# Routing a mixture-of-experts stage by a token table made on the chip, with gathered rows, folded RMS weights and an early load of half of W2

## What is computed

```python
x = x + xattn(ctx, ctx, layernorm(x), mask, wq, bq, wk, bk, wv, bv, wo, bo)
# ffn on z = layernorm(x):
xn = z * rsqrt(mean(z*z) + 1e-6) * rms_w
scores = softmax(xn @ gate_w.T)                  # 8 experts
e, s = argmax(scores), max(scores)
y = silu(xn @ W1[e] + b1[e]) @ W2[e] + b2[e]     # 256 -> 1024 -> 256
x = x + y * s
```

## Time and profile before

| | us |
|---|---|
| median of 3 runs | 1009.69 |
| lowest and highest of them | 1008.04, 1959.81 |
| the profiled execution, its time | 1013.72 |
| the profiled execution, its span (first to last instruction) | 1012.0 |
| mean granted clock of TensorE | 0.957 |

### The profile page before, as it was taken

How to read it: one execution, slowest core, us unless ns; L and a number is a source line. 1 busy time by engine, 2 the same in 40 slices (tenths; PEclk the granted TensorE clock), 3 DMA queues, 4 the chain that set the end, 5 groups by cost and what they waited for, 6 DMA issues and landing times.

```text
span 1012.0 us, 31886 instructions
## 1 busy us (share of the span) xinstructions
PE 849.3 (84%) x9355; PEld 612.3 (61%) x9356; DVE 613.6 (61%) x1906; ACT 448.0 (44%) x1121; POOL 523.5 (52%) x766
## 2 busy tenths in 40 slices
PE   1789999999999999999999999930089999999995
PEld 0456666666666666666666666610077777778773
DVE  4467777777777777777777777441044444445442
ACT  0235555555555555555555555500033333334331
POOL 0355567567667667667667667436622222232221
PEclk9999999999999999999999999955589999999998
DMA  9746765775775775775775775345222122222210
GB/s 255 184 131 164 188 185 160 179 195 149 185 200 147 187 201 144 185 206 142 189 204 142 187 206 144 76 194 215 87 58 72 59 63 76 58 71 71 66 48 7
DMA packets 124528, 143.72 MB, mean 142 GB/s; under 512 B 13274, under 2 KB 116550, under 8 KB 123464
## 3 DMA queue, kind: packets, MB, share of 16 engines
q1 hardware_dynamic: 119048, 132.15, 48.6%
q0 software_dynamic: 4896, 11.05, 3.4%
q10 hardware_dynamic: 544, 0.00, 0.0%
HBM read 100.10 MB, written 44.89 MB: 143 GB/s over the span
## 4 chain that ended last, share of the span: by engine, by line
PE 32%; issue 18%; SPq 15%; DMA 13%; POOL 12%; DVE 6%; ACT 1%; POOLq 0%; DVEq 0%; ACTq 0%
PE ps L1163 13%; DMA arena_a<-in_x 12%; PE ps L1178 10%; SPq L404 4%; SPq L399 4%; POOL arena_a L550 3%; POOL arena_b L529 3%; POOL arena_b L530 3%; PE ps L980 2%; POOL arena_a L557 2%; POOL arena_b L509 1%; SPq L365 1%; PE ps L994 1%; DVE arena_b L1297 1%; SPq L444 1%
## 5 line engine op out<-in xcount | busy, mean ns | idle before, releaser
L1315 DVE CUSTOM_DVE_ANT_0 arena_a<-ps,arena_a 112x375 bf16<-112x375 f32 x256 | 140.5, 549 | 45.5 <-PE ps L916 38.3
L697 ACT ACTIVATE arena_a<-ps 119x448 f32<-119x448 f32 (+1 forms) x256 | 131.7, 540 | 71.9 <-PE ps L942 71.3
L1163 PE MATMUL ps<-arena_b,w_parts 128*128 128x128 f16 x1680 | 148.5, 227 | 5.3 <-issue 4.3
L938 PE MATMUL ps<-arena_a 128*128 128x448 bf16 x384 | 137.3, 357 | 8.0 <-DVE arena_a L1324 5.9
L1163 PEld LDWEIGHTS ps<-arena_b,w_parts 128*128 x1680 | 118.7, 98 | 37.2 <-issue 11.2
L1315 DVE CUSTOM_DVE_ANT_0 arena_b<-ps,arena_a 112x375 bf16<-112x375 f32 x256 | 139.8, 546 | 0.0
L942 PE MATMUL ps<-arena_a 128*128 128x224 f16 x768 | 136.8, 260 | 0.0
L831 ACT ACTIVATE arena_b<-ps,b_sb 128x128 f32<-128x128 f32 x280 | 79.4, 372 | 113.3 <-PE ps L1163 113.1
L655 POOL DMA_INDIRECT out<-arena_b x35 | 35.6, 1018 | 179.8 <-DVE arena_b L1479 131.2
L1497 DVE TENSOR_SCALAR arena_b<-arena_b 128x512 f16<-128x512 f32 x70 | 30.3, 433 | 129.2 <-ACT arena_b L831 91.4
L1178 PE MATMUL ps<-arena_a,arena_b 128*128 x840 | 97.5, 273 | 4.6 <-DVE arena_b L1500 3.8
(11 more groups left out here) (170 smaller groups left out, 1510.0 us busy)
## 6 DMA issues: line engine op xcount, KB each, us to landing
arena_a<-k_spill SPq DMA_DIRECT2D x128, 192.0 KB, 3.8
arena_b<-in_L_ffn_W SPq DMA_DIRECT2D x64, 256.0 KB, 4.3
arena_a<-q_spill SPq DMA_DIRECT2D x128, 112.0 KB, 4.4
k_spill<-arena_a SPq DMA_DIRECT2D x32, 384.0 KB, 4.7
arena_b<-in_ctx SPq DMA_DIRECT2D x32, 256.0 KB
w_spill<-arena_b SPq DMA_DIRECT2D x32, 256.0 KB, 4.5
arena_a<-w_spill SPq DMA_DIRECT2D x8, 1024.0 KB, 11.7
arena_a<-in_x SPq DMA_DIRECT2D x64, 112.0 KB, 4.6
```

What stands on the lines that cost most here:

```text
L697: nc.scalar.activation(probsT[u % PROB_BUFFERS][0:n], scoreT_bank[c][0:n, 0:QUAD * T], ACT.Exp, scale=1.0 / SCALE_SCORES).then_inc(probs_r ...
L938: pe.matmul(bank[:, 0:QUAD * T], mask_keys[:, quad, c, :], max_rows[par].rearrange("p h t -> p (h t)"), start=True, stop=False)
L1163: mm = pe.matmul(ps[:, 1 + 2 * parity + f // 4, (f % 4) * P:(f % 4 + 1) * P], w1_parts[:, w_part, bass.ds(e, 1), k, f * P:(f + 1) * P].rea ...
L1315: nc.vector.tensor_tensor_reduce(out=masked_scores[r % 2], in0=shared_bank[r][0:T, 0:S], in1=mask_bias, scale=-1.0, scalar=3.4e38, op0=ALU ...
```

## The change

- Attention no longer multiplies rows by the RMS weights. They are folded into W1's scale (`w1_scale`) and the gate weights at the start. `scale_routed` goes, and `routed_factor` has two operations in place of seven (a combined epsilon makes one rsqrt of two).
- Each batch's centred row and its x1 row lie side by side in `row_tile` and are spilled together (224 KB a batch) to `rows`, in step lag 3 after `centred_ready`, in place of x1 alone (112 KB) in lag 2.
- Nothing is sorted in memory: the zero fill, `xr_all`, the 32 scatters and SP's loads of sorted rows go. The slots are worked out by a new chain of 28 linked DVE operations; then 32 one-hot comparisons (one a batch) and 32 products on PE give, for each place of each tile, the token's number. The constants for it (36 POOL instructions) are made in step 32.
- In the FFN POOL's `gather` fetches the 2 KB rows (centred row and x1) straight into `xs`, the tile that PE transposes, by the token table; a second indirect DMA fetches the scores. The copy of two token columns stands ahead of them. SP loads only b2.
- Half of W2's split parts (experts 0 to 3, 4 MB) is loaded by SP after step 17, the rest behind attention as before. W2's place in memory is a new arena, so that its first half is free during attention.

The diff, cut to its core:

```diff
-def run_steps(eng, body):
+def run_steps(eng, body, midway=None):
...
-    with eng.Fori(0, (B - 2 - PEELED_FIRST) // UNROLL) as i:
+    first, steps = PEELED_FIRST, B - 2 - PEELED_FIRST
+    if midway is not None:
+        with eng.Fori(0, EARLY_STEPS // UNROLL) as i:
+            for k in range(UNROLL):
+                body(Step(first + k, i, True))
+        midway()
+        first, steps = first + EARLY_STEPS, steps - EARLY_STEPS
+    with eng.Fori(0, steps // UNROLL) as i:
...
-            sp.wait_ge(constants, N_CONST_POOL)
-            sp.dma_start(sorted_rows.rearrange("(n p) d -> p n d", p=P),
-                         zeros.unsqueeze(1).to_broadcast([P, FFN_TILES, ROW])).then_inc(zeroed, 16)
...
-                if st.exists(2):
-                    wait_apart(sp, x1_ready, st.batch(2) + 1, sp_passed)
-                    sp.dma_start(x1_rows[bass.ds(st.batch(2), 1)].rearrange("o t d -> t (o d)"),
-                                 x1[st.parity(2)]).then_inc(x1_spilled[st.parity(2)], 16)
-            run_steps(sp, step)
+                if st.exists(3):
+                    wait_apart(sp, centred_ready, st.batch(3) + 1, sp_passed)
+                    sp.dma_start(rows[:, bass.ds(st.batch(3), 1), :].rearrange("t o d -> t (o d)"),
+                                 row_tile[st.parity(3)]).then_inc(rows_spilled[st.parity(3)], 16)
+            def load_w2(first, chunks):
+                for part in range(2):
+                    for e in range(first, first + EARLY, 2):
+                        sp.dma_start(w2_parts[:, e:e + 2, part].rearrange("p e f d -> p e (f d)"),
+                                     w2_spill[:, part, e * chunks:(e + 2) * chunks].rearrange(
+                                         "p (e c) n -> p e (c n)", e=2)).then_inc(w2_loaded, 16)
+            def load_early_w2():
+                sp.wait_ge(w2_spilled, 16 * (PEELED_FIRST + EARLY_STEPS - 1))
+                load_w2(0, B // EXPERTS)
+            run_steps(sp, step, load_early_w2)
+            sp.wait_ge(score_ready, 1)
+            sp.dma_start(score_rows, top_score).then_inc(score_spilled, 16)
...
-            def scale_routed(st):
-                b = st.batch(3)
-                wait_count(pool, xrT_ready, b)
-                pool.wait_ge(centred_ready, b + 1)
-                pool.tensor_tensor(xr_now, centred, rmsw, ALU.mult).then_inc(xr_ready, 1)
-                pool.tensor_tensor(xr_all[:, bass.ds(b, 1), 0:D].rearrange("p o d -> p (o d)"),
-                                   centred, rmsw, ALU.mult).then_inc(xr_ready, 1)
...
-            for b in range(B):
-                pool.indirect_dma_start(out=sorted_rows, out_offset=bass.IndirectOffsetOnAxis(ap=slot_of[:, b:b + 1], axis=0),
-                                        in_=xr_all[:, b, :], in_offset=None).then_inc(scattered, 16)
...
-            def gather(t, buffer, first):
+            def gather(t, buffer, nth, first):
                 if not first:
+                    pool.wait_ge(out_stored[buffer], 16 * nth)
                     pool.wait_ge(out_ready, t + 1 - FFN_UNROLL)
-                wait_apart(pool, token_ready, t + 1, pool_passed)
-                pool.indirect_dma_start(out=x1_got[buffer], out_offset=None, in_=x1_rows.rearrange("b t d -> (b t) d"),
-                                        in_offset=bass.IndirectOffsetOnAxis(ap=token_of[buffer], axis=0),
-                                        bounds_check=B * T - 1, oob_is_err=False).then_inc(x1_gathered[buffer], 16)
+                pool.tensor_copy(token_of[buffer], tokens[:, bass.ds(t, 1), :].rearrange("p o s -> p (o s)")
+                                 ).then_inc(token_copied, 1)
+                wait_apart(pool, token_copied, t + 1, pool_passed)
+                pool.indirect_dma_start(out=xs[buffer], out_offset=None, in_=rows.rearrange("t b d -> (t b) d"),
+                                        in_offset=bass.IndirectOffsetOnAxis(ap=token_of[buffer][:, 0:1], axis=0),
+                                        bounds_check=B * T - 1, oob_is_err=False).then_inc(xs_loaded[buffer], 16)
+                pool.indirect_dma_start(out=score[buffer], out_offset=None,
+                                        in_=score_rows.rearrange("t (b o) -> (t b) o", o=1),
+                                        in_offset=bass.IndirectOffsetOnAxis(ap=token_of[buffer][:, 0:1], axis=0),
+                                        bounds_check=B * T - 1, oob_is_err=False).then_inc(score_loaded[buffer], 16)
...
             for t in range(FFN_PEELED):
-                gather(t, t, True)
+                gather(t, t, 0, True)
+            gather(3, 3, 0, True)
             scatter(0, 0)
-            gather(3, 3, True)
             scatter(1, 1)
             with pool.Fori(0, FFN_LOOPS) as i:
                 for k in range(FFN_UNROLL):
                     t = FFN_UNROLL * i + FFN_PEELED + 1 + k
-                    gather(t, k, False)
+                    gather(t, k, i + 1, False)
                     scatter(t - 2, (k + 2) % FFN_UNROLL)
...
+            for b in range(B):
+                pe.wait_ge(places_ready, b + 1)
+                mm = pe.matmul(token_bank[:, 0:2 * FFN_TILES], at_place[:, b, :],
+                               in_tile_of[:, b].rearrange("p s n -> p (s n)"), start=b == 0, stop=b == B - 1)
+            mm.then_inc(tokens_found, 1)
...
+            nc.vector.tensor_scalar(rms_cols, rms_cols, (1.0 + RMS_EPS) ** -0.5, None, ALU.mult).then_inc(rms_scaled, 1)
+            dve.wait_ge(rms_scaled, 1)
+            nc.vector.tensor_scalar(w1_scale.rearrange("p (e t) -> p e t", e=EXPERTS),
+                                    rms_cols.unsqueeze(1).to_broadcast([P, EXPERTS, DT]), SCALE_W, None, ALU.mult
+                                    ).then_inc(const_dve, 1)
...
+            for b in range(B):
+                nc.vector.tensor_scalar(at_place[:, b, :], place_no[:, :], place[:, b:b + 1], None, ALU.is_equal
+                                        ).then_inc(places_ready, 1)
```

More of the change, by code:

```diff
@@ L54 @@
 PEELED_FIRST, UNROLL = 4, 2
+EARLY_STEPS = 14
 class Step:
@@ L129, in carve @@
                 n *= d
+            n += n % 2
+            if which == "a" and used["a"] + n > arena_a.shape[1]:
+                which = "b"
             at = used[which]
-            used[which] += n + n % 2
-            assert used[which] <= arena.shape[1]
+            used[which] += n
+            arena = arena_a if which == "a" else arena_b
+            assert used[which] <= arena.shape[1], (which, used)
+            n = 1
+            for d in shape:
+                n *= d
             flat = arena[0:parts, at:at + n]
@@ L170, in build @@
         eps_ln = carve("a", T, 1)
-        eps_rms = carve("a", T, 1)
+        eps_two = carve("a", T, 1)
         minus_half = carve("a", T, 1)
+        row_tile = [carve("a", T, 2 * D) for _ in range(2)]
         x_in = [carve("a", T, D) for _ in range(2)]
@@ L204, in build @@
         attT = carve("b", P, DT, T)
-        x1 = [carve("b", T, D) for _ in range(2)]
-        centred = carve("b", T, D)
-        xr_now = carve("b", T, D)
         xrT = carve("b", P, DT, T)
@@ L576, in step @@
                     split_w1(st)
-                if st.exists(3):
-                    scale_routed(st)
+                if not st.in_loop and st.base == B:
+                    route_constants()
                 if st.exists(-2):
@@ L639, in _ @@
[L639 to L644 removed]
+            pool.wait_ge(route, R_MAX)
+            pool.tensor_tensor(gate_exp, gate_logits[:, :, :], gate_max.unsqueeze(2).to_broadcast([T, B, EXPERTS]),
+                               ALU.subtract).then_inc(logits_centred, 1)
+            pool.wait_ge(rows_spilled[0], 16 * B // 2)
@@ L1412, in over_experts @@
             def over_experts(ap):
-                return ap.unsqueeze(2).to_broadcast([T, B, EXPERTS])
-            order, diff, exps, onehot, weighted, rank, counts, scan_a, scan_b = [s for s in small]
-            gmax, gsum, emax, wmax, slot_f = [small_b[0:T, i, :] for i in range(5)]
+                return ap.unsqueeze(1).to_broadcast([T, EXPERTS, B])
             dve.wait_ge(gate_copied, B)
-            link(nc.vector.tensor_reduce(gmax, gate_logits[:, :, :], AX_X, ALU.max))
-            link(nc.vector.tensor_tensor(diff[0:T], gate_logits[:, :, :], over_experts(gmax), ALU.subtract))
@@ L1437, in _ @@
-            link(nc.vector.tensor_copy(scan_a, counts))
-            a, c = scan_a, scan_b
-            for k in (1, 2, 4, 8, 16):
-                nc.vector.tensor_copy(c[:, 0:k, :], a[:, 0:k, :])
-                link(nc.vector.tensor_tensor(c[:, k:B, :], a[:, k:B, :], a[:, 0:B - k, :], ALU.add))
-                a, c = c, a
-            total = a[:, B - 1, :]
-            dve.wait_ge(route_iota, 11)
-            tiles_e, cum0, cum1, start = [small_e[:, i, :] for i in range(4)]
-            link(nc.vector.tensor_tensor(small_te, small_te, total.unsqueeze(2).to_broadcast([P, EXPERTS, B]),
-                                         ALU.is_lt))
```

(18 more changed lines are left out.)

405 lines of the change are left out of this document (212 added, 193 removed).

## The result

The changed kernel takes 1249.34 us, the median of 4 runs (1248.31 to 1250.08), against 1009.92 for the kernel before on the same chip: a ratio of 1.2378, 95% interval 1.2353 to 1.2402. It is 24% slower; 1260 had been predicted. Its profiled execution took 1248.63 us with a span of 1246.9; the traces differ by 1246.9 - 1012.0 = 234.9 us. One of the four runs of the kernel before took 1959.81 us, which hardly moves their median.

A forecast was written before the change was run, and what follows sets the result against it. Bounds: a ring of waits and transfers beside a nearly full PE in attention, PE in the FFN. Span 1012.0 + 0.4 + 10 + 10 - 39 + 270 = 1263.4; + 1.7 - 4 gives about 1260 us; range 1195 to 1325.

The forecast's parts named there:

- start: Setup before attention: two more tiny DVE operations on the chain, +0.4 us; the removed zero fill's DMA gains 0.
- spill: Attention: 112 KB more a step ahead of k_stack and x, 0.35 us in 28 steps, +10 us (0 to 15).
- early half of W2: Attention: four 1 MB DMAs stand once ahead of k_stack, q_stack, context and x, +10 us (0 to 13).
- tail of attention: Last batch's path: six POOL operations leave it, so the first routing operation comes 2.0 us earlier, at 668.3.
- gap: Between attention and FFN: 32 scatters go, routing takes 18.6 us, tile 1's rows land at 694.9, not 734.34: -39 us (-33 to -45).
- FFN: PE waits 7.5 us for each tile's gather without overlap; 8.7 us more a tile over 31 tiles, +270 us.
- rival B: FFN: the clock stays down through the outputs too, 2.1 us more a tile, 65 in all, 1325 us; chance 0.15.
- rival A: FFN: the clock stays up or recovers at once, +7.4 us a tile, 229 in place of 270, about 1220 us; chance 0.15.
- clock's term: FFN: PE's clock falls during each wait and rises during hidden products, costing 1.3 us a tile.
- ring: Attention: a loop through SP's issue of x, its landing for DVE, and POOL's masking back to SP, some 19 us a step.
- whatever is added between two of these points is added to each step: Attention: anything added between x's issue, its landing, POOL's rstd and masking, and SP's next x lengthens each step.
- Rival C, the gathers in time: FFN: rows arrive before PE asks, tiles keep 7.5 us; 991 us, or 981 if early W2 costs nothing; chance 0.08.

The follow-up runs named there:

- the dummy products: Changed kernel with 30 unused products of 512 columns on PE ahead of its wait for the rows, in the 31 tiles that stall: 1239.03 us, ratio 1.2281.
- gather-first kernels: Changed kernel with gather(t) ahead of scatter(t-4) and separate index tiles: 985.78 us, ratio 0.9777; variants build on it, with all W2 loaded behind attention 972.77 us.

## Why the prediction was right, and where it was not

Its terms against the two traces:

| part | predicted us | measured us | from |
|---|---|---|---|
| start | +0.4 | -0.8 | first q_spill 37.67 to 36.83 |
| spill, and all else in the steps | +10 | -9.4 | first to last q_spill +1.0, less the next row |
| early half of W2 | +10 | +10.4 | 29.18 - 18.8 |
| tail of attention | -2 | -1.1 | last q_spill to first routing operation |
| gap, with that tail | -39 | -38.3 | tail -1.1; then 64.1 to 26.9 us to tile 1's transposes |
| FFN | +270 | +272.2 | 247.2 to 519.4 us to the last transposes |
| end | 0 | +0.8 | last transposes to the end |
| sum | +251.4 | +234.9 | |

(The tail's row is contained in the gap's.)

*The FFN: right in its mechanism, and near in each size but the clock's.* The prediction read from one tile that POOL's gather came 3.5 us behind the transposes of its own tile and asked what would wait if these transposes needed it. Wait of PE: 7.5 predicted, 7.8 measured. PE's own part: 8.7 predicted (7.4 and 1.3 for the clock), 16.34 - 7.8 = 8.5 measured. The gather in the first position, without a word changed on PE or DVE, gives 985.78, so the cause is shown by taking it away. That PE's clock falls and comes back in every tile, by the measured rows of the tile above, was right too (rival B falls: outputs take 2.78 us, at full clock; rival A falls: the granted clock is at 0.50 in the next tile again).

*The clock's term* was read off the first tile, 5.29 and 0.69 us. That is the worst of the cases: the hidden products take 4.20 to 5.30 us in the changed kernel, 4.83 in the mean, so the clock adds 0.6 us, not 1.3. The other half of what PE's own part grew by (8.5 in place of 7.4) is a restart behind the wait: from the start of the transposes to that of the hidden products it takes 1.01 us in place of 0.52, and still 0.97 in the warm tiles of the dummy products. (The kernel before pays 0.97 to 1.02 too, once every four tiles, at the turn of its loop, so it isn't peculiar to the wait for rows.) The 0.5 us that a warm tile saves agrees with the 0.6. The first tile's rows held both in one, so the sum came out near, under one wrong name.

*The gap: right.* From the first routing operation to the token table 18.4 us against 18.6 predicted, though single links differed (of the three 1120-element operations two took 1.33 and one 0.53 where 1.2 each was taken, the 32 comparisons 5.29 where 4.8 was). Gather 0 starts 1.06 us behind its copy, a later one 0.88, as the 0.92 of the earlier trace rows had it.

*The early half of W2: right*, as bytes over 429 GB/s in a ring without slack: 10.4 us in the long step, 13.0 in the time when it is left out.

*The spill: wrong.* The step that failed is "whatever is added between two of these points is added to each step", applied to bytes. The ring consists of waits, issues and landings. In the changed kernel 112 KB more, in a DMA that nobody waits for, go with 0.08 us more up to x's issue and with no longer transfer of x, though the engines are full in that stretch; one more issue on SP cost the kernel before 0.48. That the bytes would be free in the kernel before too is argued, not shown: the run with half of them has a median step of 18.69 us against 18.70, in attention steps that are shorter than 19.07 for another reason. The Trainium skill ("DMA: Bandwidth & Descriptors", "Anatomy of one DMA — SWDGE (gpsimd) path") splits the time of a DMA that GpSimd issues in a fixed part and one for its bytes. The row store is issued by SP, for which that section has no figure; its landing has the same form, 0.3 us more for 112 KB more. What decides is what such a time delays.

*The steps* of the changed kernel are shorter than before by 0.3 us, where 0 was predicted: 19.07 to 18.77 on average, the 10.4 us of the long step left out, which is the -9.4 us of the table. The cut above finds 0.19 in x's transfer and 0.11 behind it, where POOL's two masking operations stand (0.98 us each in place of 1.04), less 0.08 in front. The gather-first kernels run at 18.68 to 18.70 with PE busy for 95% of the stretch, so there PE may be the bound and not the ring; that is argued. GpSimd's lighter load was my theory, and its run spoke against it. Some of it may not be the change at all: the profiled run of the kernel before was 4 us above its median, and no trace says in which stage. The cause stays open.

The spill's +10 that didn't come and these -9.4 are together -19.4 us; the other terms missed by +2.9 in all, and the span by -16.5. The time missed by less, 1249.34 against 1260, because the median lay 2.4 us above this span; the prediction had put it 2 to 3 us below, by the scatter of the runs before.

*Rival C, the gathers in time*, was set at 0.08 with the point from which it decides: one place further ahead in POOL's order. At that place it is still 2% slower; it takes two (the gather ahead of the scatter as well, with its tokens in tiles of their own). The kernel built that way with W2 loaded late takes 972.77 us, 3.4% faster than the kernel before and 8 us under the 981 that rival C had worked out; its steps of 18.68 us make up for tiles of 7.84.

## What to carry to other kernels

When a load's result moves from a late consumer to an early one, look up in the trace how far its issue lies ahead of the new consumer, not the old one: a gather that is free because it is used a tile later costs the whole loop when the first operation of a tile needs it. The cure is a place in a queue, and it decides the sign of the whole change here (24% slower or 2.2% faster; 3.4% with W2 left late). In a ring of DMAs count the issues and the landings that somebody waits for first; bytes that nobody waits for may cost less than their share of the bandwidth, or nothing.

## What the runs showed of the hardware

- In the loops of 7.9 us a tile, with three indirect transfers on GpSimd, ScalarE has idles of up to 3.5 us (4.4 in one run), about 40 us in 14 places, that no semaphore explains. Spreading the transfers out changes nothing, leaving out the gather of 4 bytes a row ends them. With the same three transfers at 16.3 us a tile there are none.
- 48 products of 128 columns take 4.18 us at the full clock and 5.30 at half (5.10 where the clock rises just before their end): the low clock costs this group a quarter, not a factor of two.
- A write of 3584 single elements of 4 bytes took 17.8 us from its issue on SP until its waiter went on.
- An indirect transfer of 128 rows holds GpSimd 1.0 to 1.05 us whatever it moves (4 bytes or 2 KB a row); the first of a series took 1.29.
